# Expert output rows scattered with addition into one token table, instead of stored per block and gathered again at the end

## The reference, cut to what matters

```python
logits = jnp.einsum('bsd,ed->bse', tgt, Wr) + br          # tgt = layernorm(x)
top_v, top_i = jax.lax.top_k(logits, 2)
top_w = jax.nn.softmax(top_v, axis=-1)
router_w = jnp.sum(jax.nn.one_hot(top_i, n_exp, dtype=top_w.dtype) * top_w[..., None], axis=-2)
h = jax.nn.relu(jnp.einsum('bsd,efd->bsef', tgt, W1) + b1)
o = jnp.einsum('bsef,edf->bsed', h, W2) + b2
tgt2 = jnp.einsum('bsed,bse->bsd', o, router_w)
return _layer_norm(tgt + tgt2, gamma, beta)
...
x = x + _L0_ffn_ref(_layernorm(x, axis=-1)[None], ...)[0]
```

## Time and profile before

| | us |
|---|---|
| median of three runs (lowest, highest) | 2311.53 (2309.03, 2311.81) |
| profiled execution, its own time | 2309.76 |
| span of its records | 2308.0 |
| PE busy | 2059.9 (89% of the span) |
| DVE, POOL, ACT busy | 1338.3, 914.9, 818.4 |
| mean granted clock of PE | 0.951 |

### The profile page before, as it was taken

One profiled execution on the slowest core, in us unless ns is written; L12 is line 12 of the kernel. 1 busy time (PEld: TensorE's weight loads), 2 busy tenths in 40 slices (PEclk: granted clock), 3 DMA queues, 4 the chain that ended last, 5 costly groups with the idle time before them and its releaser, 6 DMA issues. The chain is left out here.

```text
span 2308.0 us, 27801 instructions
## 1 busy us (share of the span) xinstructions
PE 2059.9 (89%) x9485; PEld 1610.2 (70%) x9485; DVE 1338.3 (58%) x2373; ACT 818.4 (35%) x1068; POOL 914.9 (40%) x805
## 2 busy tenths in 40 slices
PE   6999988899999999989999999899899199999910
PEld 5777767678888888867677677676588177888800
DVE  7578576742222222149999988889798522222158
ACT  3111121123222222235655666666444033333311
POOL 0000055546555554047777777677100111000034
PEclk9999999999999999999999999999999599999955
DMA  5222366667777777678988889884465779774163
GB/s 173 97 77 82 113 221 218 196 241 249 249 252 260 259 251 251 231 257 300 317 284 285 315 305 317 291 308 159 120 193 158 320 209 342 290 300 190 43 247 121
DMA packets 159197, 524.55 MB, mean 227 GB/s; under 512 B 33578, under 2 KB 33962, under 8 KB 157024
## 3 DMA queue, kind: packets, MB, share of 16 engines
q1 hardware_dynamic: 84752, 313.16, 38.1%
q0 software_dynamic: 70432, 195.65, 26.1%
q10 hardware_dynamic: 3888, 14.16, 1.5%
HBM read 403.66 MB, written 148.94 MB: 239 GB/s over the span
## 5 line engine op out<-in xcount | busy, mean ns | idle before, releaser
L195 PE MATMUL psum<-w_hi,xnT_hi 128*128 128x512 f32 (+1 forms) x1600 | 433.0, 406 | 12.9 <-PEq L400 6.4
L195 PE MATMUL psum<-w_lo,xnT_hi 128*128 128x512 f32 (+1 forms) x1600 | 425.3, 396 | 0.0
L195 PE MATMUL psum<-w_hi,xnT_lo 128*128 128x512 f32 (+1 forms) x1600 | 415.0, 393 | 0.0
L791 POOL DMA_INDIRECT sorted_rows<-acc x313 | 334.7, 1069 | 116.4 <-issue 85.8
L195 PEld LDWEIGHTS psum<-w_hi,xnT_hi 128*128 128x128 f32 (+1 forms) x1600 | 299.9, 191 | 84.4 <-issue 9.8
L195 PEld LDWEIGHTS psum<-w_lo,xnT_hi 128*128 128x128 f32 (+1 forms) x1600 | 299.7, 187 | 74.5
L195 PEld LDWEIGHTS psum<-w_hi,xnT_lo 128*128 128x128 f32 (+1 forms) x1600 | 296.9, 186 | 73.5
L760 DVE TENSOR_TENSOR acc<-acc 128x1024 fp32r<-128x1024 f32 x64 | 78.8, 1231 | 374.0 <-DMA split_experts<-acc 220.1
L521 ACT ACTIVATE work<-psum 128x512 f32<-128x512 f32 (+1 forms) x150 | 89.8, 599 | 546.9 <-PE psum L195 480.2
L883 POOL DMA_INDIRECT w_lo<-y_rows,sort_row x176 | 230.8, 1311 | 94.5 <-issue 57.8
L883 POOL DMA_INDIRECT w_hi<-y_rows,sort_row x176 | 235.0, 1335 | 61.9 <-issue 53.2
(11 more groups left out here) (278 smaller groups left out, 2643.5 us busy)
## 6 DMA issues: line engine op xcount, KB each, us to landing
split_experts<-acc SPq DMA_DIRECT2D x128, 512.0 KB
ring<-split_experts SPq DMA_DIRECT2D x16, 4096.0 KB, 15.1
w_raw<-in_wchunks SPq DMA_DIRECT2D x88, 512.0 KB
y_rows<-work SPq DMA_DIRECT2D x144, 256.0 KB
acc<-in_wchunks SPq DMA_DIRECT2D x64, 512.0 KB
o_rows<-o_s ACTq DMA_DIRECT2D x27, 512.0 KB
work<-local_rows SPq DMA_DIRECT2D x26, 384.0 KB
acc<-in_bias SPq DMA_DIRECT2D x10, 512.0 KB, 5.0
```

The lines of the kernel that those rows point to most:

```text
L195: i = pe.matmul(to[:rm, :], x_[:, k, m * P:m * P + rm], w_[:, s, k * HALF:(k + 1) * HALF], start=(n == 0), stop=(n == 3 * KD - 1))
L791: pool.indirect_dma_start(sorted_dram, IndirectOffsetOnAxis(ap=e_dest[:, c:c + 1], axis=0), e_rec[:, c, :], None, bounds_check=BLOCKS * P ...
```

## The change

The outputs of the experts are no longer stored block by block and gathered at the end. A table `sum_rows` of 11 x 128 rows is filled with zeros early in the kernel (22 stores of 256 KB by SP, between those of `y_rows` in chunks 2 and 3). In the expert stage ACT multiplies each output row by its router weight while it copies it (`scale=slot_w`), now into one of two buffers, and POOL scatters the 128 rows with addition into `sum_rows`, at the rows `row_at` (the token's row, or for an empty place a spare row behind them). A scatter waits for the one before it. The copy of block b waits for the scatter of block b-2.

`slot_w` (the weight by place of a block) and `row_at` are made in the routing stage. The one-hot tensors are now 32-bit and lie in the second half of `ring`, and 20 more small products make the weights. So the loads of the third and fourth ring half are started later, in the expert stage, one after the other, once the first two token gathers have landed; these two gathers are now issued in the routing stage.

The gate stage stores `x1` straight into `out`, and `beta` is added there. The last stage is gone as a stage of its own: after the last scatter POOL starts ten transfers that add the contiguous rows of `sum_rows` to `acc` on chip, DVE and ACT make the layer norm in four groups of tiles, and POOL starts ten transfers that add the result into `out`.

```diff
+LISTS = TILES_T + TILES_T % 2
...
-        x1_dram = nc.dram_tensor("x1_rows", (N, D), F32, kind="Internal").ap()
         t_dram = nc.dram_tensor("t_rows", (N, D), F32, kind="Internal").ap()
-        o_dram = nc.dram_tensor("o_rows", (TILES_T * P, D), F32, kind="Internal").ap()
+        sum_dram = nc.dram_tensor("sum_rows", ((TILES + 1) * P, D), F32, kind="Internal").ap()
...
+        def zero_steps(c, m):
+            if c not in (ZERO_CHUNK, ZERO_CHUNK + 1):
+                return ()
+            return ((m, c - ZERO_CHUNK),) + (((TILES, c - ZERO_CHUNK),) if m == TILES - 1 else ())
...
+                        for t, h in zero_steps(c, m):
+                            if (t, h) == (0, 0):
+                                sp.wait_ge(zero_made, 1)
+                            sp.dma_start(sum_dram[t * P:(t + 1) * P, h * HALF:(h + 1) * HALF], zeros).then_inc(zeroed, 16)
...
-                sp.dma_start(x1_dram[at, :], x_s[:rows(m), m % 2, :]).then_inc(x1_stored[m % 2], 16)
+                sp.dma_start(out[at, :], x_s[:rows(m), m % 2, :]).then_inc(x1_stored[m % 2], 16)
...
+        def gather_tokens(pool, b):
+            pool.indirect_dma_start(t_s[:, b % 2, :], None, t_dram, IndirectOffsetOnAxis(ap=token_at[:, b:b + 1], axis=0),
+                                    bounds_check=N - 1, oob_is_err=False).then_inc(t_in[b % 2], 16)
...
                 pool.memset(t_s[:, :, :], 0.0).then_inc(made, 1)
+                pool.wait_ge(made, 7)
+                pool.wait_ge(token_ready, 1)
+                for b in range(2):
+                    gather_tokens(pool, b)
...
-                for n in range(RING):
+                for n in range(2):
                     load_half(sp, n, n * P)
...
+                pe.wait_ge(weight_hot, 1)
+                for c in range(COLS):
+                    rm = rows(c % TILES)
+                    i = pe.matmul(bank[3][:, 0:2 * LISTS], hot_low[:rm, c, :],
+                                  hot_weight[:rm, c, :, :].rearrange("p h n -> p (h n)"), start=(c == 0), stop=(c == COLS - 1))
+                i.then_inc(weight_done, 1)
...
                 for n in range(HALVES_E):
+                    if n == 2:
+                        for i in range(2):
+                            sp.wait_ge(t_in[i], 16)
+                    if 2 <= n < RING:
+                        load_half(sp, n, n * P)
...
+                def scatter(b):
+                    pool.wait_ge(o_read, 2 * b + 2)
+                    if b >= 1:
+                        pool.wait_ge(o_added, 16 * b)
+                    pool.indirect_dma_start(sum_dram, IndirectOffsetOnAxis(ap=row_at[:, b:b + 1], axis=0), o_s[:, b % 2, :], None,
+                                            compute_op=ALU.add).then_inc(o_added, 16)
+
+                for b in range(BLOCKS_T):
+                    if b < TILES:
+                        pool.dma_start(out[b * P:b * P + rows(b), :], beta[0:1, :].to_broadcast([rows(b), D]),
+                                       accum_op=ALU.add).then_inc(x1_shifted, 16)
+                    if b + 2 < BLOCKS_T:
+                        gather(b + 2)
+                    if b >= 1:
+                        scatter(b - 1)
+                scatter(LAST)
+                pool.wait_ge(x1_shifted, 16 * TILES)
+                pool.wait_ge(rb_added, 2 * TILES)
+                pool.wait_ge(o_added, 16 * BLOCKS_T)
                 for m in range(TILES):
+                    pool.dma_start(acc[:rows(m), m, :], sum_dram[m * P:m * P + rows(m), :], accum_op=ALU.add)\
+                        .then_inc(o_got[m], 16)
+                for m in range(TILES):
+                    pool.wait_ge(scaled, m + 1)
+                    pool.dma_start(out[m * P:m * P + rows(m), :], acc[:rows(m), m, :], accum_op=ALU.add).then_inc(stored, 16)
+                pool.wait_ge(stored, 16 * TILES)
...
-                    if b >= 1:
-                        act.wait_ge(o_stored, 16 * b)
-                    else:
+                    if b >= 2:
+                        act.wait_ge(o_added, 16 * (b - 1))
+                    elif b == 0:
                         act.wait_ge(b2_ready, 1)
                     act.wait_ge(o_first, b + 1)
-                    act.activation(o_s[:, 0:HALF], bank[0], ACT.Copy).then_inc(o_read, 1)
+                    act.activation(o_s[:, b % 2, 0:HALF], bank[0], ACT.Copy, scale=slot_w[:, b:b + 1]).then_inc(o_read, 1)
...
-                    act.dma_start(o_dram[b * P:(b + 1) * P, :], o_s[:, :]).then_inc(o_stored, 16)
...
+                for g, (lo, hi) in enumerate(TAIL_GROUPS):
+                    for m in range(lo, hi):
+                        rm = rows(m)
+                        v.wait_ge(o_got[m], GOT[m] + 16)
+                        for q in range(2):
+                            i = v.bn_stats(stats[:rm, m % 2, q, :], acc[:rm, m, q * HALF:(q + 1) * HALF])
+                        link(i)
+                        link(v.bn_aggr(aggr_of[:rm, m, :], stats[:rm, m % 2, :, :]))
...
```

More of the change, by code:

```diff
@@ L1581, in _ @@
                 act.wait_ge(b2_in, 48)
-                act.activation(b2_s[:, :], o_s[:B2_K, :], ACT.Copy).then_inc(b2_hi, 1)
+                act.activation(b2_s[:, :], o_s[:B2_K, 0, :], ACT.Copy).then_inc(b2_hi, 1)
                 for b in range(BLOCKS_T):
@@ L1592, in _ @@
                 output(LAST)
-                act.wait_ge(o_stored, 16 * BLOCKS_T)
+                for g, (lo, hi) in enumerate(TAIL_GROUPS):
+                    act.wait_ge(var_ready, g + 1)
+                    act.activation(std_of[:, lo:hi], var_of[:, lo:hi], ACT.Sqrt).then_inc(std_ready, 1)
+                    act.wait_ge(rstd_ready, g + 1)
+                    for m in range(lo, hi):
+                        act.wait_ge(centred, m + 1)
+                        o = acc[:rows(m), m, :]
+                        act.activation(o, o, ACT.Copy, scale=rstd_of[:rows(m), m:m + 1]).then_inc(scaled, 1)
             @block.vector
@@ L1631, in _ @@
                     hidden_lo(b)
+                for g, (lo, hi) in enumerate(TAIL_GROUPS):
+                    for m in range(lo, hi):
+                        rm = rows(m)
[4 more added lines that the diff above has]
+                        link(v.bn_aggr(aggr_of[:rm, m, :], stats[:rm, m % 2, :, :]))
+                    s, std, r, w = var_of[:, lo:hi], std_of[:, lo:hi], recip_of[:, lo:hi], w_of[:, lo:hi]
+                    v.tensor_scalar(s, aggr_of[:, lo:hi, 1], EPS, None, ALU.add).then_inc(var_ready, 1)
+                    for m in range(lo, hi):
+                        o = acc[:rows(m), m, :]
+                        v.scalar_tensor_tensor(out=o, in0=o, scalar=aggr_of[:rows(m), m, 0:1], in1=gamma_bc[:rows(m), :],
+                                               op0=ALU.subtract, op1=ALU.mult).then_inc(centred, 1)
+                    v.wait_ge(std_ready, g + 1)
+                    link(v.reciprocal(r, std))
+                    link(v.tensor_tensor(w, r, r, ALU.mult))
+                    link(v.tensor_tensor(w, w, s, ALU.mult))
+                    link(v.tensor_scalar(w, w, -0.5, 1.5, ALU.mult, ALU.add))
+                    v.tensor_tensor(rstd_of[:, lo:hi], w, r, ALU.mult).then_inc(rstd_ready, 1)
             @block.tensor
```

196 lines of the change are left out of this document (74 added, 122 removed).

## The result

The changed kernel takes 2298.61 us (median of four runs, 2296.37 to 2306.08), the kernel before 2311.67 (four runs, 2309.03 to 2315.40). The ratio is 0.9949, with a 95% interval of 0.9926 to 0.9971: faster by half a per cent, 13 us instead of the 51 forecast, and outside the range 2243 to 2280. In a later set of runs on one chip it was 2296.23 against 2316.20, ratio 0.9910 (0.9894 to 0.9926), so 20 us: a gain either way, and less than half of the forecast.

The account below looks back on a forecast made before the run. PE was taken to set the expert stage's time, a chain of other work the last stage's; start -12.5, experts +4 and end -43.1 sum to -51.6 us, so about 2260 us, range 2243 to 2280.

Parts of the forecast that it names:

- The start, -12.5: Routing to first expert product: gathers issued early into idle DMA engines, that product at 1839.2 instead of 1851.71, -12.5 us.
- The end, -43.1: Last stage: twenty adding transfers back to back at 2.8 us, 63.0 us in all against 106.15, -43.1 us.
- DVE's case: Last stage: adding transfers cost little over plain ones, DVE sets the end; stage -54.5 us, about 2249; chance 0.15.
- Zeros and scale operand, 0: Zero stores under busy PE and ACT's scale operand in the experts: both priced at nothing; zeros 7.3 us without cover.
- The experts, +4 with bounds -3 and +20: Expert stage: -3 us for two buffers plus 7 us of stall, +4 us, bounds -3 and +20.
- I take 7 us of stall, with 0 and 23 as bounds: First ten expert blocks: 14.0 us of transfers against 12.85 of PE work, partly covered, 7 us of stall.
- After the tenth block ... no stall: Later expert blocks: 4.2 us of transfers against 12.85, 11.2 with ring loads, so no stall.
- The -3 for the second buffer: Expert stage: two `o_s` buffers spare PE waits for `hT_lo`, 6.4 us of which 3.4 stay; booked -3 us.
- backlog of ten blocks: First ten expert blocks: gathers come behind adding transfers, PE waits in each; experts +20, about 2275 us; chance 0.17.
- the scatters' chain: Expert stage: each scatter waits for the one before; slower if above 15.0 us per block, about 2336 at 16; chance 0.04.
- landings over 13 us: Sign in the profile after: scatters landing over 13 us after their issue would show the scatters' chain sets the pace.
- The reserve of two blocks: Expert stage: the gather runs two blocks ahead, and that reserve was to cover part of the up to 12 us shortfall.

Follow-up runs that it names:

- e5: The kernel before, with only ring halves 2 and 3 loaded later, in the expert stage after the first two gathers land: 2307.8 us, ratio 0.9967.
- e6: e2 with DVE's operations from `used` to `end_of` moved into its wait for the list products: 2271.0 us, ratio 0.9813.
- e10: e2 plus even tiles' sums loaded plainly, DVE's wait filled, one gather ahead of the stage border, groups of 3, 3, 3, 1: 2267.8 us, ratio 0.9809.
- e1: The changed kernel run once more, unaltered, beside the kernel before on one chip: 2296.2 us, ratio 0.9910.
- e12: e2's order and e9's two tables together on the changed kernel, odd blocks' rows never added: 2263.6 us, ratio 0.9779.
- e9: Changed kernel, odd blocks' scatters to a second table never added, each scatter waiting for the one two before: 2270.3 us, ratio 0.9823.
- e2: Changed kernel with each block's scatter moved behind the gather of four blocks on in POOL's loop: 2270.2 us, ratio 0.9809.
- e3: Changed kernel with scatters that write instead of adding, so sums are the last writer's rows: 2265.2 us, ratio 0.9777.

## Why the prediction was wrong

*The start, -12.5:* measured -11.1, for the reason given, four ring halves in front of the gathers (e5). Two details were off. Twenty 32-bit one-hot products take 4.45 us, 0.22 each, not 3.2, which is most of the missing 1.4 us. And I let DVE's chain alone set the end, where the landing of the gathers at the border does so as well (e6, e10).

*The end, -43.1:* measured -40.2. Twenty adding transfers back to back, 2.65 us each instead of 2.8, 3 us less; what is more by 6 us lies ahead of the first sum load (7.0 us from the last copy at 2238.38 to its issue, for the 5.1 forecast) and behind the last transfer, for which I had 0.4: its packets end at about 2299.6, 4.7 us before the span does. DVE's case rested on 1.31 us a transfer, which no adding transfer showed.

*Zeros and scale operand, 0:* nothing seen of the zeros. With the scale operand a copy of ACT takes 0.69 us instead of 0.60, on an engine that doesn't set the pace.

*The experts, +4 with bounds -3 and +20:* measured +40.6, and +36.3 in e1. This is the step that failed, in the sentences "I take 7 us of stall, with 0 and 23 as bounds" and "After the tenth block ... no stall". The -3 for the second buffer could not be told from the spread (e12 is 4.0 below the kernel before, in its shortest execution). The stall was sized by averages, transfer work per block against a block's time, and such a sum says that little is lost. The loss is one of latency. I had named the chain myself, a gather queued behind a scatter that waits for its block's copy and for the scatter before, but priced its two halves apart: the gathers' lateness as a backlog of ten blocks, and the scatters' chain only as a pace of over 15 us in every block. I sized that chain with the middle landing of 9.2 us, where scatters beside a ring half took 12.6 to 16.2; landings over 13 us were my own sign for it. And it does harm below the 15.0 us a block that I asked of it (the stage came to 14.5 a block). In the case shown a scatter that lands in 14.23 us is late for the next one by only 2.7 us; the gather behind it had already lost 6.3 us to the copy and 1.9 to the scatter's issue, and itself takes 18. So PE stops for 3 to 6 us once in three blocks, in the blocks after the tenth as well, as long as ring halves are loaded (the last is issued at 2129, the last stop ends at 2119.75). And the stops have a second price that no term had: the granted clock is at the low level after the longer ones (0.50 against 1.00), and the busy time of PE grew by 14.0 of the 40.6 us. The reserve of two blocks, which I let cover part of the shortfall, was what the new order had used up: POOL's new order, laid beside PE's timeline of before, would have shown 24 us turning into 13 or 16 against landings that reach 19.8. None of the cases that I gave chances was this one: the backlog came nearest in size (+20), the chain in kind. That the time still fell is owed to the other two terms; the forecast of a faster kernel holds, its size doesn't.

Shown are that taking away the chain (e9) or the order (e2) takes away most of the loss, and that with both away PE waits for gathers 1.0 us in all and no loss can be told (e12). How the 14 us of clock would fall without the idle time isn't separable here; they went away together. Why the runs with one order differ by up to 9.5 us in this stage is open. Which share of a landing of 18 us is the ring's and which the adding transfers' was not measured apart.

## What to carry to other kernels

Where a transfer that nobody needs soon must wait (for a copy, for the one before it), put every urgent transfer of that queue ahead of it: the same transfers issued in another order were worth 26 us here. Judge a prefetch by its reserve, from issue to use, against the longest landing beside the other traffic, not by the engines' mean load; and price stops of PE at their length and about half as much again for the clock after them (against the kernel before 14.0 us of busy time beside 26.5 of idle time, 12.6 beside 23.7 in e1, 3.8 beside 7.5 in e9; but 5.7 beside 5.8 in e3, so it is a rough price). Two large loads that nobody needs yet, started ahead of a small one that everybody waits for, cost 11 us in the profiles, 7 in the medians.

## What I had not expected of the hardware

An adding transfer from DRAM to the chip or from the chip to DRAM cost about the same, 2.65 us a tile in throughput, twice a plain one's 1.31 (in 2247:2275, with both kinds, 198 GB/s at a DMA share of 1.06, in 2275:2300, with outputs nearly alone, 189 at 0.95). A scatter with addition landed in about 6 us where the queue was clear, and in up to 16.2 beside a ring half. The plain one of e3 gained mostly in the former: 3.3 us alone for 6.15, and still 15.4 beside a half for 16.2, as its chain of waits shows:

```profile
1907.11 15.42 DMA sum_rows<-o_s,row_at
...
2202.81 3.33 DMA sum_rows<-o_s,row_at
```

And a stage's border held the engines until the packets of POOL's gathers had passed (e6, e10), though no wait in the kernel's text at that place names them.
